# A fused decoder block: two heads share 32 rows of turned queries and keys, and the heads' outputs are packed by DMA and divided there

## The chip, the cores and the metric

The kernel runs on one core of one Trainium2 chip. The metric is the device time of one execution in microseconds (us), the median of several. A core has TensorE (PE in the profile, with its weight loads as PEld), VectorE (DVE), ScalarE (ACT), GpSimd (POOL) and SyncE (SP), which here only issues DMAs. Each engine works through its own instructions in order and waits at semaphores.

## The reference

One decoder block on 16 sequences of 256 tokens, width 256, 16 heads of 16, all in f32:

```python
# self-attention
k = layernorm_per_head(x @ Wk.T); q = layernorm_per_head(x @ Wq.T); v = x @ Wv.T
q, k = q * 256**-0.25, k * 256**-0.25
att = softmax(causal(q k^T));  x1 = layernorm(x + (att v) @ Wo.T + bo)
# cross-attention: queries of x1, keys and values of ctx, RoPE on q and k
att = softmax(Q K^T / sqrt(16));  x2 = layernorm(x1 + (att V) @ Wo + bo)
# mixture of 8 experts, 2 chosen per token, then the last layernorm
top2 = top_k(x2 @ router.T); y = sum(p_e * (gelu(x2 @ w1_e + b1_e) @ w2_e + b2_e))
```

## The kernel before

The kernel is written by hand, engine by engine, with explicit semaphores. Attention runs over 32 blocks: blocks 0 to 15 are the sequences' self-attention, 16 to 31 their cross-attention. Time is counted in quarters `q`; a block has four, and each engine's program is one loop over `q` with a fixed list of steps for each `r = q % 4`. The table of constants near L46 says how many quarters after a block's start each of its steps stands (`block_at`, `group_at`); several blocks are in flight at once. So the order of work on each engine is written out and does not depend on times.

One quarter handles one group of four heads. PE computes that group's scores (`score`), the weighted values of an earlier group (`weigh`) and the turned scores of another (`score_T`), from which ACT takes the exponentials (`weights`). DVE takes the maxima of the scores, in two halves (`maxima`, L1075); PE may not begin the next score before both are taken, nor the quarter's turned score before the first. PE reads the scores' operands from `qkT`, where the queries and keys lie turned (features on rows), 32 rows to a head, 16 of them used and one more for the maximum (queries) or a 1 (keys). To get there the rows of `qkn` are scaled (`scale_heads`) or rotated (`rotate`, `sum_turn`, `lay_out`) into the padded tile `pad`, then turned by PE in four jobs of four transposes (`turn_qk`, L645) and drained by ACT (`drain_turned`).

The values carry a column of ones, so `weigh` gives each head's outputs with their sum in row 16 of its 32 rows. PE turns these back (`turn_o`, L655, eight transposes), DVE inverts the sums and multiplies (`divide`, L1204 and L1208), PE turns the result again (`turn_on`, L669, four transposes), ACT drains it, and PE projects it (`project_o`, L681). DVE then adds the residual (L1219).

Most PE results go through two PSUM banks used in turn (the ring, `ring_places`); a job waits until the job two before it is drained. SP issues all plain DMAs on one queue: the maxima into `qkT` (`lay_max`, L382, four a block), the inputs (`load_xin`, `load_xb`), and in blocks 2 to 13 the zero rows of the experts' buffer (`lay_pads`, L392, two copies of 1,496 KB a block). POOL masks, adds biases and scatters the tokens; its tables for RoPE's bias are made at the start (`prepare_rope`). Behind the last block stand the experts (L792, L803), which the change does not touch.

Of the kernel before, what the change touches and what calls it, by code (L numbers as in the profile page):

```python
# [73 lines left out]
def ring_places():  # L74
# [7 lines left out]
    for q in range(QUARTERS):  # L82
        r = q % 4
        if r == 0:
            place("maxT", block_at(q, MAXT_AT))
            n = block_at(q, QK_AT)
            place("x1T", n, n is not None and crossed(n))
        elif r == 1:
            place("k23", block_at(q, TURN_K23))
        elif r == 2:  # L90
            place("o0", block_at(q, OUT_AT))
        else:
            place("onT", block_at(q, PROJECT_AT))
# [3 lines left out]
        elif r == 1:  # L97
            place("q23", block_at(q, TURN_Q23))
            place("qk1", block_at(q, QK_AT + 1))
        elif r == 2:  # L100
            place("o1", block_at(q, OUT_AT))
            place("v", block_at(q, V_AT))
            place("q01", block_at(q, TURN_Q01))
            n = block_at(q, TURN_X2)
            place("x2T", n, n is not None and crossed(n))
        else:
            place("k01", block_at(q, TURN_K01))
# [11 lines left out]
def decoder_block(nc, x, xT, ctxT, wqk_self, wv_self, wo_self, wq_x, wk_x, wv_x, wo_x, bo_self, bo_x,  # L119
# [4 lines left out]
    with ExitStack() as ctx:  # L124
# [30 lines left out]
        gv = sb("gv", [P, 4])  # L155
        cs = sb("cs", [P, 2, NT, 2, D])
# [8 lines left out]
        big = sb("big", [P, KC * NE * F])  # L165
        qkT = big[:, 0:6144].rearrange("p (b q g t) -> p b q g t", b=3, q=2, g=NG)
        pad = big[:, 6144:8192].rearrange("p (t q h d) -> p t q h d", t=NT, q=2, h=H)
# [10 lines left out]
        on = sb("on", [P, NT, E])  # L178
        onT = sb("onT", [P, KC, T])
# [3 lines left out]
        rec = sb("rec", [P, NT, H])  # L183
# [57 lines left out]
        bqk = pflat[:, 512:512 + 2 * E].rearrange("p (q e) -> p q e", q=2)  # L241
        bv = pflat[:, 1024:1024 + E]
        bvT = pflat[:, 1280:1280 + E].rearrange("p (c t) -> p c t", c=KC)
        gb = pflat[:, 1536:1536 + 2 * NT * 2 * D].rearrange("p (a t q d) -> p a t q d", a=2, t=NT, q=2)
        gp = pflat[:, 1792:1792 + 4 * P].rearrange("p (j i d) -> p j i d", j=4, i=GRP)
        turned_bias = pflat[:, 2304:2304 + 2 * E].rearrange("p (q e) -> p q e", q=2)
# [12 lines left out]
        early_in, late_in = sem("early_in"), sem("late_in")  # L259
# [3 lines left out]
        gp_ready, gp_pe, gv_ready = sem("gp_ready"), sem("gp_pe"), sem("gv_ready")  # L263
# [43 lines left out]
        def bc(ap, n):  # L307
            return ap.unsqueeze(len(ap.shape)).to_broadcast(list(ap.shape) + [n])
# [1342 lines left out]
```

## Time and profile before

| | |
|---|---|
| median of 3 runs | 1244.41 us (1242.04 to 1250.48) |
| the profiled execution | 1243.51 us, span 1241.8 us, mean granted clock 0.926 |
| PE busy | 1096.5 us, 88% |
| DVE busy | 801.8 us, 65% |
| ACT busy | 575.2 us, 46% |
| POOL busy | 274.3 us, 22% |
| attention, self blocks at full pace | about 78 to 348 us |
| attention, cross blocks at full pace | about 430 to 790 us |
| experts and last layernorm | from about 915 us |

Busy time is the sum of an engine's instructions; the span goes from the first to the last instruction of the execution. A share of the whole span mixes stages, so the table by stage and the timelines of single blocks tell more than the total. Registers, branches and the issuing of DMAs are not counted as busy. The granted clock is given as a share of TensorE's full speed.

### The profile page before, as it was taken

To read this page: it belongs to the slowest core of one execution; us is meant where nothing else is said; L and a number is where in the kernel's file an instruction comes from. 1 tells how busy PE (TensorE), PEld (TensorE's weight loads), DVE (VectorE), ACT (ScalarE), POOL (GpSimd) and SP (SyncE) were. 2 spreads that over 40 slices of the span, in tenths; PEclk is the share of its full clock that TensorE was granted. 3 is DMA by queue.
4 is the path that set the end of the run, shared out by engine and by line. 5 is a ranking of instruction groups with operands and counts; after the bars stand their busy time and mean duration, and the time that the engine had idled before them with its cause. 6 is when DMAs were issued, how large, how long until landed. Compare 5 with 4: busy or idle time off the path is not lost.

```text
span 1241.8 us, 29875 instructions
## 1 busy us (share of the span) xinstructions
PE 1096.5 (88%) x11181; PEld 801.0 (65%) x11181; DVE 801.8 (65%) x1935; ACT 575.2 (46%) x937; POOL 274.3 (22%) x311
## 2 busy tenths in 40 slices
PE   5899999999999899999999999888539999999920
PEld 3456666666666666666666666555439999999920
DVE  5647777778788787687777786753624444444447
ACT  2356666666655555555455554544212222222214
POOL 4022223232222200003030302202132222222210
PEclk9889999999999999999899998876669999999975
DMA  6104644635531000101010100001057767777654
GB/s 229 63 22 160 203 150 143 201 126 183 169 118 29 10 11 19 44 10 48 10 46 11 47 15 33 29 11 38 22 173 209 211 220 213 212 220 214 194 235 188
DMA packets 94651, 139.31 MB, mean 112 GB/s; under 512 B 11216, under 2 KB 68944, under 8 KB 93104
## 3 DMA queue, kind: packets, MB, share of 16 engines
q1 hardware_dynamic: 87888, 114.98, 29.8%
q0 software_dynamic: 6624, 22.42, 4.7%
q8 instruction: 93, 1.52, 0.5%
q14 instruction: 46, 0.38, 0.1%
HBM read 76.56 MB, written 60.29 MB: 110 GB/s over the span
## 4 chain that ended last, share of the span: by engine, by line
PE 75%; DVE 14%; issue 5%; ACT 3%; DMA 2%; POOL 1%; SPq 1%; ACTq 0%; POOLq 0%; DVEq 0%
PE PS L792 10%; PE PS L803 10%; PE PS L534 9%; PE PS L555 8%; PE PS L645 5%; PE PS L503 5%; PE PS L614 4%; PE PS L610 4%; DVE part L1075 3%; PE PS L681 3%; PE PS L628 2%; PE PS L510 2%; PE PS L655 2%; PE PS L669 2%; PE PS L506 2%
## 5 line engine op out<-in xcount | busy, mean ns | idle before, releaser
L1075 DVE TENSOR_REDUCE part<-PS 128x6 f32<-128x768 f32 (+1 forms) x256 | 272.5, 1087 | 114.2 <-PE PS L510 65.2
L871 ACT ACTIVATE pT<-PS 128x768 f32<-128x768 f32 (+1 forms) x256 | 220.8, 914 | 96.7 <-PE PS L534 96.7
L1536 POOL TENSOR_SCALAR_AFFINE_SELECT pT<-pT 128x512 f32<-128x512 f32 x128 | 87.6, 689 | 294.2 <-ACT pT L871 291.2
L534 PE MATMUL PS<-big 17*128 17x256 f32 (+1 forms) x2048 | 142.0, 393 | 9.7 <-DVE part L1075 6.6
L792 PEld LDWEIGHTS PS<-oT,big 128*128 128x128 f32 x1136 | 139.3, 194 | 5.2 <-ACT oT L982 1.6
L555 PE MATMUL PS<-pT,vaug 128*32 128x256 f32 (+1 forms) x2048 | 130.9, 375 | 12.0 <-DVE sq L1178 4.6
L792 PE MATMUL PS<-oT,big 128*128 128x128 f32 x1136 | 139.9, 277 | 1.0 <-ACT oT L982 1.0
L534 PEld LDWEIGHTS PS<-big 17*128 17x128 f32 x2048 | 98.7, 194 | 57.7 <-DVE part L1075 28.2
L803 PE MATMUL PS<-w2s,qkn 128*128 x568 | 134.4, 380 | 0.0
L1553 POOL DMA_INDIRECT xs_dram<-rows_all,posi x64 | 64.3, 1004 | 298.8 <-DVE posi L1331 282.9
L982 ACT ACTIVATE oT<-PS 128x256 f32<-128x256 f32 x71 | 27.2, 383 | 192.5 <-PE PS L781 192.5
L1572 POOL DMA_INDIRECT p_dram<-pT,rowid x71 | 68.1, 959 | 209.7 <-DVE rowid L1433 202.4
L803 PEld LDWEIGHTS PS<-w2s,qkn 128*128 128x128 f32 x568 | 102.4, 190 | 11.3 <-issue 0.3
L555 PEld LDWEIGHTS PS<-pT,vaug 128*32 128x32 f32 x2048 | 57.2, 112 | 60.3 <-issue 35.3
L882 ACT ACTIVATE oT<-PS 128x256 f32<-128x256 f32 x128 | 49.0, 383 | 98.9 <-PE PS L555 98.4
L1417 DVE TENSOR_TENSOR qkn<-PS,b1T 128x512 f32<-128x512 f32 x71 | 49.1, 691 | 65.2 <-PE PS L792 65.2
L645 PE MATMUL PS<-ident,big 128*128 128x128 f32 x512 | 84.5, 289 | 6.7 <-DVE on L1208 4.2
L1427 DVE TENSOR_TENSOR pT<-PS,w_self 128x256 f32<-128x256 f32 x71 | 30.1, 424 | 87.8 <-PE PS L803 87.8
L503 PE MATMUL PS<-big 16*128 16x256 f32 x1024 | 76.3, 413 | 9.4 <-ACT big L916 6.1
L645 PEld LDWEIGHTS PS<-ident,big 128*128 128x128 f32 x512 | 55.0, 143 | 42.7 <-issue 32.3
L614 PE MATMUL PS<-w_self,xin 128*128 128x512 f32 x128 | 68.4, 664 | 1.7 <-DVE w_self L1017 1.3
L503 PEld LDWEIGHTS PS<-big 16*128 16x128 f32 x1024 | 48.0, 190 | 27.4 <-ACT big L916 11.9
(166 smaller groups left out, 1603.6 us busy)
## 6 DMA issues: line engine op xcount, KB each, us to landing
big<-w SPq DMA_DIRECT2D x71, 512.0 KB
xs_dram<-zrow SPq DMA_DIRECT2D x24, 1496.0 KB, 9.0
oT<-xs_dram SPq DMA_DIRECT2D x71, 136.0 KB, 3.5
xin<-xT SPq DMA_DIRECT2D x16, 256.0 KB, 2.8
w2s<-w POOLq DMA_DIRECT2D x1, 4096.0 KB, 12.9
xb<-x SPq DMA_DIRECT2D x16, 256.0 KB, 10.6
xin<-ctxT SPq DMA_DIRECT2D x16, 256.0 KB, 2.8
big<-p_dram SPq DMA_DIRECT2D x4, 1024.0 KB, 7.9
```

The lines of the kernel that those rows point to most:

```text
L503: ins = pe.matmul(o, q, a[r0:r0 + D, 1, g, :], start=True, stop=True)
L534: ins = pe.matmul(o, keys, a[r0:r1, 0, g, q0:T], start=True, stop=True)
L555: ins = pe.matmul(o[PADDED * i:PADDED * (i + 1), q0:T], vaug[:, n % 4, kt, GRP * g + i, :], pT[:, k % 2, i, kt * T:kt * T + T - q0], start ...
L614: ins = pe.matmul(o, a[:, c, t * P:(t + 1) * P], w_qk[:, c, :], start=(c == 0), stop=(c == KC - 1))
L645: ins = pe.transpose(ring_slot(job)[:, j * T + t * P:j * T + (t + 1) * P], src, ident[:])
L792: ins = pe.matmul(moe_bank(1, j % 2)[:, f * P:(f + 1) * P], w1s[:, j % W1_BUFFERS, c, f * P:(f + 1) * P], xsT[:, j % 2, c * P:(c + 1) * P] ...
L803: ins = pe.matmul(moe_bank(3, j % 2)[:, 0:E], hact[:, j % 2, c * P:(c + 1) * P], w, start=(c == 0), stop=(c == FC - 1))
L871: act.activation(pT[:, k % 2, 2 * half:2 * half + 2, 0:wide], src, ACT.Exp).then_inc((exp_a, exp_b)[half], 1)
L1075: dve.tensor_reduce(dst, src, AX.X, ALU.max, negate=True).then_inc((max_a, max_b)[half], 1)
L1536: pool.affine_select(d, d, [[0, 2], [0, 2], [1, P]], ALU.is_ge, 0.0, base=0, channel_multiplier=-1).then_inc(masked, 1)
L1553: pool.indirect_dma_start(out=xs_dram, out_offset=bass.IndirectOffsetOnAxis(ap=posi[:, batch_index(last), c:c + 1], axis=0), in_=rows_all[ ...
L1572: pool.indirect_dma_start(out=p_dram, out_offset=bass.IndirectOffsetOnAxis(ap=rowid[:, o, 0:1], axis=0), in_=ye[:, o], in_offset=None).the ...
```

## The change

Queries and keys are now turned without padding: 16 heads of 16 fill 128 rows twice, so four transposes turn the queries of a block and four its keys (`turn_qk` reads `qkn` itself). Two heads share each strip of 32 rows. ACT drains each turned bank twice, once for each of the two heads of a strip, with a factor per row that is 1 (or the gain) on the head's own 16 rows and 0 on the other's (`within`, `gvb`); the keys get a 1 on one of the other's rows (`beyond`), and the maximum goes there in the queries. `score` contracts 32 rows.

The two transposing steps of the outputs and ACT's drain between them are gone. SP packs the outputs by 16 DMAs a block (`pack`): eight bring the 16 output rows of each head into a dense tile `packed[:, 0]`, eight bring the 16 rows of its sums (the ones columns give the sum in rows 16 to 31 alike) into `packed[:, 1]`. DVE inverts and multiplies there (`divide`), and the projection reads the tile as it is.

Some steps move: `divide` to quarter 3, the residual to the next quarter 0, `scale_heads` to quarter 1, `sum_turn` to quarter 2, `lay_out` to quarter 3, `turn_x1` three quarters earlier. At the start, the values' projection waits for four loads (`mid_in`), the bias tables are made later, and ACT no longer waits for them.

```diff
-QK_AT, V_AT, SQUARE_AT, VAR_AT, CHAIN_AT, SCALE_AT = 0, 2, 2, 3, 4, 6
-TURN_Q01, TURN_K01, TURN_Q23, TURN_K23 = 6, 7, 9, 9
-SUM_AT, LAY_AT = 3, 6
+QK_AT, V_AT, SQUARE_AT, VAR_AT, CHAIN_AT, SCALE_AT = 0, 2, 2, 3, 4, 5
+TURN_X1, TURN_Q, TURN_K = -3, 6, 7
+SUM_AT, LAY_AT = 2, 3
-OUT_AT, PROJECT_AT, LN_AT = 18, 19, 21
+PACK_AT, PROJECT_AT, LN_AT = 16, 19, 21
...
+            def pack(n, b):
+                if n is None:
+                    return
+                if b == 0 and n >= 1:
+                    await_filled(sp, ("wo", n - 1))
+                for g in range(2 * b, 2 * b + 2):
+                    await_drained(sp, ("pv", (n, g)))
+                for k in range(2):
+                    for i in range(GRP):
+                        r0, r1 = PADDED * i + D * k, PADDED * i + D * b
+                        sp.dma_start(packed[r1:r1 + D, k], oT[r0:r0 + D, n % 2, 2 * b:2 * b + 2, :]
+                                     ).then_inc(packed_in[n % 2], 16)
...
                 load_xb(block_at(q, MAXT_AT + 1))
+                pack(block_at(q, PACK_AT), 0)
+                pack(block_at(q, PACK_AT + 1), 1)
                 n = block_at(q, MAXT_AT)
                 if n is not None:
                     lay_pads(n)
...
             def project_o(n):
-                await_drained(pe, ("onT", n))
+                pe.wait_ge(divided, n + 1)
...
             def drain_turned(...):
+                for b in range(2):
+                    dst = qkT[:, n % 3, qk, 2 * b:2 * b + 2, :].rearrange("p g t -> p (g t)")
+                    if crossed(n):
+                        factor, term = within[:, b:b + 1], beyond[:, b:b + 1] if qk else none[:]
+                    else:
+                        factor, term = gvb[:, 0, b, qk:qk + 1], gvb[:, 1, b, qk:qk + 1]
+                    ins = act.activation(dst, ring_slot(job), ACT.Identity, bias=term, scale=factor)
+                ins.then_inc(drained_by(job), 1)
...
-            def divide(n, t):
+            def divide(n):
                 if n is None:
                     return
-                job = (("o0", "o1")[t], n)
-                await_filled(dve, job)
-                m = ring_slot(job).rearrange("p (h d) -> p h d", d=PADDED)
-                dve.reciprocal(rec[:, t, :], m[:, :, D]).then_inc(rec_ready, 1)
-                dve.wait_ge(rec_ready, next(n_rec))
-                if t == 0 and n >= 1:
-                    await_filled(dve, ("onT", n - 1))
-                dve.tensor_tensor(on[:, t, :].rearrange("p (h d) -> p h d", d=D), m[:, :, 0:D],
-                                  bc(rec[:, t, :], D), ALU.mult).then_inc(drained_by(job), 1)
+                dve.wait_ge(packed_in[n % 2], 256 * (n // 2 + 1))
+                dve.reciprocal(packed[:, 1], packed[:, 1]).then_inc(inverted, 1)
+                dve.wait_ge(inverted, n + 1)
+                dve.tensor_tensor(packed[:, 0], packed[:, 0], packed[:, 1], ALU.mult).then_inc(divided, 1)
...
                 if r == 0:
+                    residual(block_at(q, PROJECT_AT + 1))
...
                 elif r == 2:
                     maxima(group_at(q, SCORE_AT), 0)
-                    divide(block_at(q, OUT_AT), 0)
                     maxima(group_at(q, SCORE_AT), 1)
-                    scale_heads(block_at(q, SCALE_AT))
-                    lay_out(block_at(q, LAY_AT))
-                    divide(block_at(q, OUT_AT), 1)
+                    for t in range(NT):
+                        sum_turn(block_at(q, SUM_AT), t)
                     choose_second(block_at(q, SECOND_AT))
                 else:
                     maxima(group_at(q, SCORE_AT), 0)
                     maxima(group_at(q, SCORE_AT), 1)
                     combine(block_at(q, MAXT_AT - 1))
+                    divide(block_at(q, PROJECT_AT))
                     variances(block_at(q, VAR_AT))
-                    for t in range(NT):
-                        sum_turn(block_at(q, SUM_AT), t)
-                    residual(block_at(q, PROJECT_AT))
+                    lay_out(block_at(q, LAY_AT))
                     combine_weights(block_at(q, RANK_AT))
```

Three places of the resulting order follow. PE, quarters 2 and 3 of a self-attention block. Before (L655 and L669 turn outputs, L645 queries and keys, L628 projects values, L681 outputs):

```order
L510 MATMUL PS<-big 128x256 x4
L655 MATMUL PS<-ident,oT 128x128 x4
L555 MATMUL PS<-pT,vaug 32x256 x4
L555 MATMUL PS<-pT,vaug 32x128 x4
L534 MATMUL PS<-big 128x256 x4
L534 MATMUL PS<-big 128x128 x4
L655 MATMUL PS<-ident,oT 128x128 x4
L628 MATMUL PS<-w_self,xin 128x256 x4
L645 MATMUL PS<-ident,big 128x128 x4
L494 MATMUL PS<-identb,strips 128x2x32 x16
L506 MATMUL PS<-big 128x128 x4
L510 MATMUL PS<-big 128x256 x4
```

Now (L661 turns queries, L645 projects values):

```order
L529 MATMUL PS<-big 128x256 x4
L661 MATMUL PS<-ident,qkn 128x128 x4
L574 MATMUL PS<-pT,vaug 32x256 x4
L574 MATMUL PS<-pT,vaug 32x128 x4
L553 MATMUL PS<-big 128x256 x4
L553 MATMUL PS<-big 128x128 x4
L645 MATMUL PS<-w_self,xin 128x256 x4
L512 MATMUL PS<-identb,strips 128x2x32 x16
L525 MATMUL PS<-big 128x128 x4
L529 MATMUL PS<-big 128x256 x4
```

Three groups of four transposes became one here; between the projection of the values and the next score none is left.

DVE, from quarter 2 of a self-attention block to the next quarter 0. Before (L1204 and L1208 divide, L1152 sums the squares, L1219 is the residual):

```order
L1075 TENSOR_REDUCE part<-PS 128x2x3
L1204 RECIPROCAL rec<-PS 128x16
L1208 TENSOR_TENSOR on<-PS,rec 128x256
L1075 TENSOR_REDUCE part<-PS 128x2x3
L1141 TENSOR_TENSOR big<-qkn,chain 128x32x16 x2
L1204 RECIPROCAL rec<-PS 128x16
L1208 TENSOR_TENSOR on<-PS,rec 128x256
L1075 TENSOR_REDUCE part<-PS 128x2x3 x2
L1082 TENSOR_TENSOR part<-part 128x16
L1152 TENSOR_REDUCE vv<-sq 128x64
L1219 TENSOR_TENSOR y<-PS,xb 128x512
```

Now:

```order
L1133 TENSOR_TENSOR qkn<-qkn,chain 128x512 x2
L1070 TENSOR_REDUCE part<-PS 128x2x3 x4
L1077 TENSOR_TENSOR part<-part 128x16
L1188 RECIPROCAL packed<-packed 128x512
L1190 TENSOR_TENSOR packed<-packed 128x512
L1142 TENSOR_REDUCE vv<-sq 128x64
L1200 TENSOR_TENSOR y<-PS,xb 128x512
```

The scaling moved ahead of quarter 2's maxima, and one division of 512 columns stands behind the four maxima of quarters 2 and 3.

SP's queue, one self-attention block with zero rows. Before:

```order
L382 DMA big<-nmaxT 1x4x256 x4
L392 DMA xs_dram<-zrow 128x11x272 x2
L375 DMA xb<-x 128x2x256
L367 DMA xin<-xT 128x2x256
```

Now:

```order
L388 DMA big<-nmaxT 4x256 x4
L400 DMA packed<-oT 16x512 x8
L410 DMA xs_dram<-zrow 128x11x272 x2
L380 DMA xb<-x 128x2x256
L400 DMA packed<-oT 16x512 x8
L372 DMA xin<-xT 128x2x256
```

Eight packing copies stand ahead of the zero rows and eight behind them and `xb`.

## Rows read from the trace of the kernel before

**Rows 1.** Table by stage: us, busy us per engine, PEclk, DMA share, GB/s.

```profile
250.00:350.00 100.00, 98.97 (x1386) 64.84 (x1386) 76.56 (x151) 66.86 (x107) 30.22 (x41) 1.00 0.46 150
600.00:700.00 100.00, 95.17 (x942) 65.07 (x935) 73.51 (x180) 52.70 (x81) 21.36 (x20) 0.97 0.11 35
```

**Rows 2.** Timeline of PE, self-attention block: start us, us, engine, line, what.

```profile
190.38 1.98 PE L614 MATMUL PS<-w_self,xin 128*128 128x512 f32 x4
...
204.22 0.29 PE L494 MATMUL PS<-identb,strips 32*128 32x64 bf16 x16
...
205.18 0.66 PE L669 MATMUL PS<-ident,on 128*128 128x128 f32 x4
...
207.42 0.66 PE L645 MATMUL PS<-ident,big 128*128 128x128 f32 x4
207.91 1.89 PE L681 MATMUL PS<-w_self,onT 128*128 128x256 f32 x8
209.83 0.30 PE L494 MATMUL PS<-identb,strips 32*128 32x64 bf16 x16
...
212.81 0.70 PE L614 MATMUL PS<-w_self,xin 128*128 128x512 f32 x1
```

**Rows 3.** Timeline of DVE, the same block.

```profile
191.60 0.49 DVE L1112 TENSOR_SCALAR chain<-vv 128x66 f32<-128x66 f32 x1
...
193.84 1.82 DVE L1075 TENSOR_REDUCE part<-PS 128x6 f32<-128x768 f32 x2
...
197.52 0.60 DVE L1130 SCALAR_TENSOR_TENSOR shift<-vv,chain 128x2 f32<-128x2 f32 x1
...
211.81 0.88 DVE L1227 BATCH_NORM_STATS2 bst<-y 128x6 f32<-128x256 f32 x2
```

**Rows 4.** Groups on DVE, by shape: xcount | busy us, mean ns | idle.

```profile
L1185 DVE TENSOR_TENSOR qkn<-qkn,sq 128x512 f32<-128x512 f32 x32 | 20.9, 695 | 0.0
...
L1204 DVE RECIPROCAL rec<-PS 128x16 f32<-128x16 f32 x64 | 15.9, 248 | 17.8 <-PE PS L655 17.7
...
L1292 DVE RECIPROCAL prob<-odds 128x4 f32<-128x4 f32 x7 | 1.2, 178 | 0.2
...
L1292 DVE RECIPROCAL prob<-odds 128x2 f32<-128x2 f32 x2 | 0.3, 166 | 0.1
```

**Rows 5.** Timeline of PE, cross-attention: two successive blocks' first rows.

```profile
675.09 1.13 PE L610 MATMUL PS<-wx_q,x1T 128*128 128x256 f32 x4
...
702.88 1.13 PE L610 MATMUL PS<-wx_q,x1T 128*128 128x256 f32 x4
```

**Rows 6.** Timeline of DVE in that block: rotation and the maxima behind it.

```profile
677.17 0.69 DVE L1176 TENSOR_TENSOR qkn<-PS,cs 128x512 f32<-128x512 f32 x1
...
678.44 2.34 DVE L1075 TENSOR_REDUCE part<-PS 128x4 f32<-128x1024 f32 x2
```

**Rows 7.** Table by stage, slices of 1 us in a self-attention block.

```profile
192.00:193.00 1.00, 1.00 (x33) 0.63 (x32) 0.93 (x3) 0.63 (x2) 0.67 (x2) 1.00 0.33 119
202.00:203.00 1.00, 1.00 (x6) 0.87 (x6) 1.00 (x3) 0.98 (x2) 0.66 (x1) 1.00 0.45 147
```

**Rows 8.** One line's instructions, L375 (the loads of xb): issue to landing.

```profile
DMA to landing us min/median/max: 2.8/10.6/11.3
```

**Rows 9.** Timeline of SP's queue: the copies of the maxima, as issued.

```profile
211.62 1.86 SPq L382 DMA_DIRECT2D big<-nmaxT  x3
```

**Rows 10.** Timeline of PE at idles, and in the last block.

```profile
427.85 0.86 PE L555 MATMUL PS<-pT,vaug 128*32 128x256 f32 x16 [1.91 <-DVE sq L1178]
...
791.40 1.15 PE L503 MATMUL PS<-big 16*128 16x256 f32 x16 [1.34 <-DVE part L1075]
...
797.76 1.96 PE L503 MATMUL PS<-big 16*128 16x256 f32 x16 [1.96 <-ACT big L916]
...
881.70 3.78 PE L681 MATMUL PS<-wx_o,onT 128*128 128x256 f32 x8 [0.69 <-ACT onT L854]
```

**Rows 11.** Timeline of ScalarE at the start.

```profile
21.80 0.60 ACT L903 ACTIVATE vaug<-PS 128x512 f32<-128x512 f32 x1 [6.40 <-POOLq L1510]
```

More of the change, by code:

```diff
@@ L85, in ring_places @@
             place("maxT", block_at(q, MAXT_AT))
[L86 to L89, printed above, removed]
         elif r == 2:
-            place("o0", block_at(q, OUT_AT))
-        else:
-            place("onT", block_at(q, PROJECT_AT))
+            place("qT", block_at(q, TURN_Q))
+        elif r == 3:
+            place("kT", block_at(q, TURN_K))
         place("pv", group_at(q, WEIGH_AT))
@@ L275, in decoder_block @@
         masked = sem("masked")
-        rec_ready = sem("rec_ready")
+        packed_in = sems("packed_in", 2)
+        inverted, divided = sem("inverted"), sem("divided")
         xb_ready, y_link = sem("xb_ready"), sem("y_link")
@@ L308, in bc, with head @@
             return ap.unsqueeze(len(ap.shape)).to_broadcast(list(ap.shape) + [n])
+        def head(g, i):
+            b, c = divmod(g, 2)
+            return 8 * c + 2 * i + b
         def ring_slot(job):
@@ L380, in lay_max @@
                 await_drained(sp, ("maxT", n))
-                for i in range(GRP):
-                    sp.dma_start(qkT[PADDED * i + D:PADDED * i + D + 1, n % 3, 0],
-                                 nmaxT[GRP * i:GRP * i + GRP, :]).then_inc(max_in, 16)
+                for g in range(NG):
+                    first = D if g < 2 else 0
+                    sp.dma_start(qkT[first:P:PADDED, n % 3, 0, g], nmaxT[g:H:NG, :]).then_inc(max_in, 16)
+            def pack(n, b):
[10 more added lines that the diff above has]
+                                     ).then_inc(packed_in[n % 2], 16)
             def lay_pads(n):
@@ L399, in _ @@
             load_xin(0)
-            for dst, src in ((small[:], tables), (w_v, wv_self), (gb[:, 0], gains), (gb[:, 1], shifts),
-                             (w_o, wo_self), (wx_q[:], wq_x), (wx_k[:], wk_x), (wx_v[:], wv_x),
-                             (wx_o[:], wo_x), (bo[:, 0], bo_self), (bo[:, 1], bo_x), (bqk[:, 0], bq_x),
+            for dst, src in ((small[:], tables), (w_v, wv_self), (gb[:, 0], gains), (gb[:, 1], shifts)):
+                sp.dma_start(dst, src).then_inc(mid_in, 16)
+            load_xin(1)
+            for dst, src in ((w_o, wo_self), (bo[:, 0], bo_self), (wx_q[:], wq_x), (wx_k[:], wk_x),
+                             (wx_v[:], wv_x), (wx_o[:], wo_x), (bo[:, 1], bo_x), (bqk[:, 0], bq_x),
                              (bqk[:, 1], bk_x), (bv, bv_x), (cs[:], rope), (rw[:], router)):
                 sp.dma_start(dst, src).then_inc(late_in, 16)
-            load_xin(1)
             for q in range(QUARTERS):
@@ L630, in project_v, with turn_qk @@
                 ins.then_inc(filled_by(job), 1)
-            def turn_qk(name, n, qk, half):
+            def turn_qk(name, n, qk):
                 if n is None:
@@ new lines, in prepare @@
+                dve.wait_ge(gv_taken, 1)
+                for b in range(2):
+                    dve.tensor_scalar(gvb[:, 0, b], gv[:, 0:2], within[:, b:b + 1], None, ALU.mult)
+                    dve.tensor_scalar(gvb[:, 1, b, 0:1], gv[:, 2:3], within[:, b:b + 1], None, ALU.mult)
+                    ins = dve.tensor_scalar(gvb[:, 1, b, 1:2], gv[:, 3:4], within[:, b:b + 1], beyond[:, b:b + 1],
+                                            ALU.mult, ALU.add)
+                ins.then_inc(gv_ready, 1)
```

242 lines of the change are left out of this document (97 added, 145 removed).

## The prediction, written before the changed kernel was run

> **What bounds the kernel now.** I read the table by stage first. In the self-attention stage TensorE (PE) is busy 98.97 of 100 us at full clock, VectorE (DVE) 76.56; in the cross-attention stage 95.17 and 73.51 [rows 1]. So both stages run at PE's pace, and DVE has about a quarter of its time free. The timeline of PE gives the pace: one block of self-attention takes 22.43 us (from 190.38 to 212.81, [rows 2]), one of cross-attention 27.79 us [rows 5]. A block is four quarters; each has one score group, one weighing and one turned score group, and fixed extra work. Between the blocks' 12 full self periods (78 to 348 us) and 13 full cross periods (430 to 790 us) lie 3 mixed ones. The expert part after 915 us is not touched.
>
> **What goes.** Each block loses 20 of its 28 PE transposes of 128x128: 8 of 16 for queries and keys, 8 of the outputs, 4 of the divided outputs. Four of them take 0.49 us behind a turned score group (207.42 to 207.91, [rows 2]) and about 0.6 behind a score. So 5 x 0.55 = 2.7 us, PE's own work falling to 19.7 us in a self block. The score matmuls contract 32 rows for 16; their columns stay, and I cost that at nothing: they take the same row strips, and the 17-row turned scores run at the 16-row ones' pace. If PE stayed saturated, 28 x 2.7 would be 76 us. ScalarE gains a second pass over each turned bank and loses one drain; it has 30% free and I cost it at nothing while PE waits elsewhere.
>
> **What comes: the division.** Before, DVE inverted 16 sums per partition, twice a block, 248 ns each, and multiplied 256 elements [rows 4]. Now the sums lie in a 128x512 tile, each repeated over the rows of its head, and one reciprocal inverts all 512 per partition. The trace has no such size. Its small ones are 166 ns for 2 elements, 178 for 4 and 248 for 16 [rows 4]: 5.8 to 6 ns per element, while an ordinary operation takes 695 ns for 512 [rows 4], near 1 ns. The bounds are 0.7 us (a reciprocal streams like any operation, the slope being start-up) and 7.9 us (16 to 512 in proportion). I take the straight line through the three rows: 0.15 + 512 x 0.0058 = **3.15 us**, and 0.7 for the multiplication: 3.85 us, where 1.34 stood.
> The Trainium skill, in "VectorE: DVE Perf Modes", section "First, the fixed hardware budget", says that reciprocal is an iterative divide with a repeat count of 8. The trace agrees with an iterative operation; eight cycles per element would be more than its rows give, and is a rival below.
>
> **Where it lands.** The division stands in quarter 3, behind both maxima of that quarter's scores, and the output projection of the same quarter waits for it. I lay out a self block from the start of quarter 3's score (t=0), with steps from [rows 2] and [rows 3].
> PE: score to 0.96; turn, weigh, turned score (as 205.18 to 207.42) to 3.2; then it needs the division.
> DVE: two maxima (193.84 to the next step, 1.73) from 1.1 to 2.85, combining to 3.0, reciprocal to 6.15, multiplication to 6.85. PE waits **3.7 us**. Projection (1.92, 207.91 to 209.83) to 8.8.
> Then DVE's residual waits for that projection (8.9 to 9.6), and its queue is a chain: score maxima of quarter 0 (from 9.95), moments 1.3, second maxima, first half of the rsqrt chain 2.24 (191.60 to 193.84) to 15.25; the first maxima of quarter 1 end at 16.1. PE, after score and weighing of quarter 1, would start its turned score at 15.45, so it waits 0.75. DVE: second maxima, rest of the chain 2.55 (to the end of 197.52's row), scaling 1.25, to 20.8. PE is at the query turn at 19.9 and waits 0.95. The rest runs at PE's pace; quarter 3 begins again at 24.95. A self block without other delay: 19.7 + 3.7 + 0.75 + 0.95, or 24.95 by the layout: **25.0 us, +2.6**.
> Cross block: the same wait is 0.1 + 2.27 (two maxima, 678.44 onwards) + 3.85 - 2.67 (PE's turn, weigh, turned score) = 3.6; in quarter 1 DVE's queue (moments, chain, rotation 1.27, from 677.17 to 678.44, [rows 6]) makes PE wait about 1.1. 27.8 - 1.2 (small idles before) - 2.7 + 3.6 + 1.1 = 28.6, **+0.8**; 13 of them 10 us. The 3 mixed ones: +0.5 each.
>
> **The copies that pack.** 16 DMAs a block are added on SP's queue, 8 in quarter 0 ahead of the zero rows (two copies of 1.5 MB, 12 self blocks have them), 8 in quarter 1 behind these and behind xb. SP's issues take 0.62 us apiece and the four of the maxima start 1.8 us after quarter 0 (211.62 against 209.83, [rows 2, 9]). So the zero rows start at 1.8 + 12 x 0.62 = 9.2. They fill the DMA engines for 10 us (eleven slices from 192 to 203, the nine between at 1.0, [rows 7]), and xb, issued behind them, lands after 10.6 us in the median against 2.8 when alone [rows 8]: the queue works in turn. So the zero rows end at about 19.6, xb and the last eight copies (256 KB each) at about 22.2. DVE reaches the division at 16.15 + 3.0 = 19.1. It waits 3.1, then 3.85 and the projection: a block of **28.0 us, +5.6**, 12 of them 67 us. Bounds of this wait: nothing (a block of 25.0) and 10 us (queue full, all issues held back). In cross blocks nothing is ahead; the copies land near 16 of a needed 22.
>
> **The clock.** PE now idles 3.7 us and more in one piece in every block. Before, of five idles of 1.7 us or more outside the last part (ending at 20.1, 32.2, 70.7, 427.8 and 797.8), four were followed by the lower level (1.2 GHz), as before 797.76, where an idle of 1.96 us made a score of 1.15 us take 1.96 (791.40 and 797.76, [rows 10]); one of 1.91 us at 427.85 was not [rows 10]. The stretches lasted 3 to 21 us. If it falls, the projection costs 1.9 more (3.78 for 8 matmuls at 881.70, [rows 10]), the next score 0.9, in cross blocks the logits 0.9: 3.3 on average, all on the path. Bounds 0 and 3.3 a block; I take 0.7 x 3.3 = 2.3, since idles are longer than those of the rows: 28 x 2.3 = 64 us.
>
> **The ends.** At the start ScalarE no longer waits 6.4 us for POOL's rope tables [rows 11], and the first value projection waits for 4 late loads, not 16: -9 (-5 to -13). At the end the last block's 8 copies (5.0), their landing (2.8) and 3.85 stand where 12 transposes and two drains stood: +6 (0 to 12).
>
> **Sum.** 67 + 10 + 1.5 + 64 - 9 + 6 = +140 on the profiled execution's 1243.5, so 1383. The median of the runs shown is 1244.4, 1 us above; no difference to the forecast. One per cent, 12 us, is what a measurement can tell from no change.
>
> **Rivals and chances.**
> A, the forecast, 0.60: **1383**, its own range 1340 to 1430.
> B, 0.14: all waits come, but the clock stays up. For it: from 82 to 600 us the granted clock hardly fell; against it: those blocks had no idle of 2 us. 1243.5 + 76 = 1319.
> C, 0.08: the packed copies are not held up by the zero rows. For it: they are small and many rings may let them by; against: xb's landing. 12 x 3.1 less: 1346, or 1282 with the clock up too.
> D, the other side, 0.10: the reciprocal streams at about 1 ns per element. Place: quarter 3's division; price 0.7 for 3.15 us. PE's wait falls from 3.7 to 1.2 and the block to 22.5 (self) and 26.1 (cross), and with idles that short the clock stays. With the copies in time: 0 + 13 x (-1.7) - 3 and the mixed blocks -6, about 1212; with them late (+3.1 in 12 blocks) 1249. For it: three rows of tiny size are thin evidence; against: all three lie on one line, with six times the slope of any other operation. Leaving the clock out, it decides the sign from about 1.8 us for the reciprocal downwards. 0.06 for the first, 0.04 for the second.
> E, 0.06: eight cycles per element. A cycle is what an ordinary operation needs per element, (695 - 166)/510 = 1.04 ns [rows 4], so 0.15 + 512 x 8.3 ns = 4.4 us, 1.2 more in 28 blocks: 1383 + 34 = 1417. Against: the rows say 5.6 cycles. The Trainium skill, "VectorE: DVE Perf Modes", can be read so.
> F, 0.02: the change pays in full, 2.7 us a block and 9 at the start: 1244 - 85 = 1159. It needs a division that hides; nothing on PE stands between.
> Range: B's 1319 and E's 1417 are in, D, F and half of C out: **1300 to 1430**. Faster: D's first case and F, 0.08. Same: D's second, 0.04. Slower: 0.88.
>
> **What would show it.** Right: a 128x512 reciprocal near 3.15 us; PE's largest wait on the projection, released by DVE's multiplication, 3 to 4 us in cross blocks and 6 to 7 in self blocks; DVE waiting for packed copies in blocks 1 to 12 alone; granted clock at 0.5 after those idles; self blocks of 28 to 31 us and cross blocks near 31. Wrong: a reciprocal below 2 us, periods under 22.4 and 27.8, or packed copies landing before the maxima end. A clock that stays at 1.0 gives B.

## The result and the profile after

| | before | after |
|---|---|---|
| median | 1243.22 us (1237.72 to 1250.48, 4 runs) | 1403.43 us (1401.06 to 1410.35, 4 runs) |
| profiled span | 1241.8 us | 1402.0 us |
| mean granted clock | 0.926 | 0.878 |
| PE busy | 1096.5 us | 1053.8 us |
| DVE busy | 801.8 us | 889.3 us |

The change makes the kernel slower: the ratio is 1.1281, 95% interval [1.1241, 1.1321], where 1383 us and a range of 1300 to 1430 were forecast. PE has less to do and the kernel still takes 160 us more, so the loss is idle time and low clock. The table by stage of the kernel after, same stretches and columns as [rows 1] (the stretch, its length, busy us of PE, PEld, DVE, ACT, POOL, then the granted clock, DMA share and GB/s):

```profile
250.00:350.00 100.00, 65.53 (x870) 40.75 (x870) 60.92 (x97) 42.80 (x69) 19.92 (x28) 0.84 0.42 128
600.00:700.00 100.00, 83.33 (x780) 57.27 (x781) 74.83 (x143) 45.48 (x68) 3.82 (x3) 0.90 0.13 36
```

In self-attention PE falls from 98.97 to 65.53 busy us of 100 and DVE falls too, so neither is the bound: they wait for each other. The waits of the kernel after name the place (engine, line, whom it waited for; us in total, times, longest):

```profile
PE PS L674 <- DVE packed L1190: 187.0, 31, 12.0
...
DVE y L1200 <- PE PS L674: 74.5, 32, 3.7
...
DVE packed L1188 <- DMA packed<-oT: 76.1, 15, 10.6
```

PE waits before each projection (L674) for the multiplication (L1190), 6 us on average. DVE itself waits before the reciprocal (L1188) for the copies in 15 blocks: 59.2 of the 76.1 us are in the twelve blocks with zero rows, 4.9 each, 0.8 in one more, and 16.1 in the last two blocks of all, where no later block is left to work on. One such block, first on DVE, then on PE, then on SP's queue (start, duration; in brackets the idle before and what ended it):

```profile
342.38 1.82 DVE L1070 TENSOR_REDUCE part<-PS 128x6 f32<-128x768 f32 x2 [3.60 <-PE PS L529]
344.31 0.17 DVE L1077 TENSOR_TENSOR part<-part 128x16 f32<-128x16 f32 x1
348.67 3.35 DVE L1188 RECIPROCAL packed<-packed 128x512 f32<-128x512 f32 x1 [4.19 <-DMA packed<-oT]
352.06 0.69 DVE L1190 TENSOR_TENSOR packed<-packed 128x512 f32<-128x512 f32 x1
352.67 1.21 DVE L1142 TENSOR_REDUCE vv<-sq 128x64 f32<-128x1024 f32 x1
```
```profile
343.60 0.94 PE L553 MATMUL PS<-big 32*128 32x256 f32 x16
352.81 3.55 PE L674 MATMUL PS<-w_self,packed 128*128 128x256 f32 x8 [8.27 <-DVE packed L1190]
356.29 0.30 PE L512 MATMUL PS<-identb,strips 32*128 32x64 bf16 x16
```
```profile
334.22 1.47 SPq L410 DMA_DIRECT2D xs_dram<-zrow  x2
335.74 3.59 SPq L380 DMA_DIRECT2D xb<-x  x1
339.43 7.84 SPq L400 DMA_DIRECT2D packed<-oT  x8
```

Read backwards, the chain is this: the projection starts at 352.8 because the multiplication ended then, this because of 3.35 us of reciprocal, and this because the last copies landed at 348.7, after SP had issued the eight of them from 339.4 to 347.3. The zero rows fill the DMA engines until about 344 (their share is 1.03 to 1.08 in the slices of 2 us from 336 to 344), but from 346 to 348 it is 0.28 and the last of the eight are still being issued: the copies end with their issuing. Behind the zero rows and `xb` one issue takes 0.98 us, where sixteen in a cross block took 0.63 each (10.03 us from 548.13). The projection then takes 3.55 us where it took 1.92 [rows 2]. The table by stage of this stretch shows the clock (columns as above, the clock third from the end):

```profile
345.00:349.00 4.00, 0.00 (x0) 0.00 (x0) 0.33 (x1) 1.12 (x2) 2.53 (x3) 1.00 0.36 90
349.00:350.00 1.00, 0.00 (x0) 0.00 (x0) 1.00 (x1) 0.00 (x0) 0.00 (x0) 0.58 0.56 191
350.00:356.00 6.00, 3.19 (x8) 2.50 (x8) 3.85 (x3) 0.00 (x0) 0.00 (x0) 0.50 0.01 3
356.00:358.00 2.00, 2.00 (x44) 1.02 (x46) 1.29 (x2) 0.32 (x1) 0.00 (x0) 1.00 0.01 4
```

Behind its idle PE is at the lower level (0.50, 1.2 GHz), and it is back at the higher one (2.4 GHz) as the projection ends; only the projection pays. A cross block has the same without the copies: idle 3.80 us, projection 3.57 us.

```profile
754.38 3.34 DVE L1188 RECIPROCAL packed<-packed 128x512 f32<-128x512 f32 x1
757.76 0.69 DVE L1190 TENSOR_TENSOR packed<-packed 128x512 f32<-128x512 f32 x1
```
```profile
753.56 1.15 PE L553 MATMUL PS<-big 32*128 32x256 f32 x16
758.51 3.57 PE L674 MATMUL PS<-wx_o,packed 128*128 128x256 f32 x8 [3.80 <-DVE packed L1190]
```

To place the 160 us I took, in each kernel, the starts of ScalarE's drain of the turned maxima (one per block) and their distances. S is the mean of the ten distances in self-attention from block 3 to 13, C that of the thirteen in cross-attention from 17 to 30; "to block 3" runs from the span's start, "last" from block 31's drain to the end.

| | to block 3 | S | 13 to 17 | C | 30 to 31 | last | span |
|---|---|---|---|---|---|---|---|
| before | 121.5 | 22.43 | 103.0 | 28.31 | 31.2 | 393.8 | 1241.8 |
| after | 131.9 | 32.31 | 123.4 | 30.61 | 26.3 | 399.4 | 1402.0 |

So of +160: 10 x 9.88 = 99 in these self blocks, 10 up to block 3, 20 from block 13 to 17 (the mixed blocks and the self blocks beside them), 13 x 2.30 = 30 in cross blocks, -5 and +6 at the end.

### The profile page after: what moved, and what is told of

It reads as the page before. It is cut to its first block, busy times and chain, and to the rows that moved or that the text cites. A ratio compares the mean times of both kernels' runs of the same rounds, so it can differ in the third digit from the quotient of the medians.

```text
span 1402.0 us, 28744 instructions
## 1 busy us (share of the span) xinstructions
PE 1053.8 (75%) x10541; PEld 766.7 (55%) x10541; DVE 889.3 (63%) x1879; ACT 560.1 (40%) x905; POOL 265.8 (19%) x309
## 4 chain that ended last, share of the span: by engine, by line
PE 52%; DVE 29%; SPq 8%; issue 5%; DMA 4%; ACT 2%; POOL 0%; DVEq 0%; ACTq 0%; POOLq 0%
PE PS L785 9%; PE PS L796 9%; PE PS L674 8%; DVE part L1070 8%; DVE packed L1188 7%; SPq L400 7%; PE PS L522 5%; PE PS L553 4%; PE PS L574 4%; PE PS L627 3%; PE PS L645 3%; DMA packed<-oT 2%; DVE packed L1190 2%; PE PS L661 1%; DVE qkn L1133 1%
## 5 line engine op out<-in xcount | busy, mean ns | idle before, releaser
L553 PE MATMUL PS<-big 32*128 32x256 f32 (+1 forms) x2048 | 137.5, 383 | 31.5 <-issue 28.3
L1516 POOL TENSOR_SCALAR_AFFINE_SELECT pT<-pT 128x512 f32<-128x512 f32 x128 | 81.8, 639 | 413.0 <-ACT pT L851 409.1
L1188 DVE RECIPROCAL packed<-packed 128x512 f32<-128x512 f32 x32 | 107.1, 3348 | 76.1 <-DMA packed<-oT 76.1
L674 PE MATMUL PS<-w_self,packed 128*128 128x256 f32 x128 | 58.8, 639 | 125.1 <-DVE packed L1190 125.1
L553 PEld LDWEIGHTS PS<-big 32*128 32x128 f32 x2048 | 96.6, 189 | 77.2 <-issue 45.9
L818 ACT ACTIVATE nmaxT<-PS 16x256 f32<-16x256 f32 x32 | 11.9, 373 | 301.7 <-PE PS L589 301.7
L674 PEld LDWEIGHTS PS<-w_self,packed 128*128 128x128 f32 x128 | 40.2, 329 | 137.0 <-DVE packed L1190 128.3
L964 ACT ACTIVATE oT<-PS 128x256 f32<-128x256 f32 x71 | 27.3, 384 | 194.1 <-PE PS L774 194.1
L674 PE MATMUL PS<-wx_o,packed 128*128 128x256 f32 x128 | 52.7, 585 | 61.9 <-DVE packed L1190 61.9
L522 PE MATMUL PS<-big 32*128 32x256 f32 x1024 | 79.9, 429 | 6.3 <-ACT pT L851 5.0
```

What stands on the lines that cost most here:

```text
L522: ins = pe.matmul(o, q, a[r0:r1, 1, g, :], start=True, stop=True)
L553: ins = pe.matmul(o, keys, a[r0:r1, 0, g, q0:T], start=True, stop=True)
L674: ins = pe.matmul(ring_slot(job)[:, t * E:(t + 1) * E], packed[:, 0, c, t * P:(t + 1) * P], w[:, c, :], start=(c == 0), stop=(c == KC - 1))
L1188: dve.reciprocal(packed[:, 1], packed[:, 1]).then_inc(inverted, 1)
L1516: pool.affine_select(d, d, [[0, 2], [0, 2], [1, P]], ALU.is_ge, 0.0, base=0, channel_multiplier=-1).then_inc(masked, 1)
```

## The experiments

Twelve kernels ran. With the first eight the kernel before took 1270.5 and 1267.7 us in place of 1243, with the last four 1244.4 and 1246.9; so each is told by its ratio to the kernel before beside it, and S and C are from its profile. Three of them, e1_plain, e3_both and e9_late_plain, leave the inversion of the sums out, so their outputs are not the block's; their instructions are otherwise the same, with the same 71 expert tiles.

C is less safe than S: `e2_zero_last` differs from the kernel after in nothing that runs in a cross block, and its C is 33.85 against 30.61. Its trace shows where most of that lies. In the profiles of the first eight kernels ScalarE has 10 to 14 idles of up to 6.4 us, all in cross-attention behind block 17, that no event of the core ended (the profile says "remote"), as here in e2_zero_last:

```profile
661.84 0.38 ACT L863 ACTIVATE oT<-PS 128x256 f32<-128x256 f32 x1 [4.36 <-remote]
```

They sum to 1.9 to 3.0 us per cross block, 2.98 in e2_zero_last, and the profiles of the kernel before, the kernel after and the last four have none. What they are is not shown; they came with the runs in which the kernel before was slower too, though it has no profile there. S has none of them. C is compared between kernels of one group alone, and with these idles in mind.

| kernel | ratio, 95% interval | S | C |
|---|---|---|---|
| after | 1.1281 [1.1241, 1.1321] | 32.31 | 30.61 |
| e1_plain | 1.0351 [1.0262, 1.0441] | 29.41 | 28.51 |
| e2_zero_last | 1.0889 [1.0793, 1.0984] | 27.32 | 33.85 |
| e3_both | 0.9697 [0.9608, 0.9786] | 22.83 | 28.23 |
| e4_turn_only | 1.0206 [1.0117, 1.0296] | 25.07 | 31.47 |
| e5_fill | 1.0452 [1.0409, 1.0495] | 25.47 | 31.09 |
| e6_late | 1.0225 [1.0194, 1.0255] | 24.65 | 30.28 |
| e8_slots | 1.0051 [1.0016, 1.0086] | 22.97 | 31.28 |
| e9_late_plain | 0.9635 [0.9593, 0.9676] | 22.12 | 27.78 |
| e10_slots_scale | 0.9851 [0.9813, 0.9890] | 22.84 | 27.87 |
| e11_spread | 0.9765 [0.9723, 0.9806] | 22.68 | 26.66 |
| e12_spread_slots | 1.0131 [1.0092, 1.0170] | 22.77 | 29.23 |
| e14_spread_residual | 0.9689 [0.9653, 0.9726] | 22.72 | 26.03 |

### The reciprocal, the zero rows, and both

```diff
 # e1_plain, and in e3_both
-dve.reciprocal(packed[:, 1], packed[:, 1])
+dve.tensor_scalar(packed[:, 1], packed[:, 1], 1.0, None, ALU.mult)
 # e2_zero_last, and in e3_both: behind pack(block_at(q, PACK_AT + 1), 1)
-n = block_at(q, MAXT_AT)
+n = block_at(q, MAXT_AT + 1)
 if n is not None:
     lay_pads(n)
```

e1_plain. 

> The changed kernel with an ordinary multiplication by 1 in place of the reciprocal (so the sums are not inverted). Theory (the division's length is on the path of every block): DVE's step falls from 3.35 to 0.7 us or less, 2.7 in each of 31 blocks, about 85 us; PE's idle in cross blocks falls from 3.8 to about 1.1 and the clock stays up there, another 20 to 30: 1285 to 1300. The late copies stay in the self blocks. Rival (the reciprocal only fills time in which PE waits for something else): less than 40 us, 1365 or more.

e2_zero_last. 

> The changed kernel, only that the zero rows are issued behind the second eight packing copies, not ahead of them. Theory (the copies wait in SP's queue behind the zero rows): DVE's wait of 76 us for packed copies goes, self blocks fall from 32 to 27 or 28 us, 1325 to 1340. Rival (16 copies a block are late by their own issuing, 0.6 us and more each): the wait stays over 40 us, 1370 or more.

e3_both. 

> Both edits together (no inversion of the sums, zero rows last). Theory: 76 and 85 us go and the clock stays up, which gives 40 to 60 more: 1190 to 1215, below the kernel before. Rival (other parts of the change cost too: the second drains, 32-row scores): 1244 or more.

Measured 1319.2, 1388.9 and 1234.4 us beside 1270.5 of the kernel before. By their ratios, on the 1243.2 us of the kernel before in the result, that is 1287, 1354 and 1206: the first and the third lie in their theories' ranges. The second lies 14 us above its own and 16 below its rival's, though its self blocks fell to 27.3 as the theory said. Without the long reciprocal a self block is 2.9 us shorter, without the copies' delay 5.0, without both 9.5: more than the sum, because only then the clock stays up (one matmul of the self-attention projections has a median of 634 ns in e1_plain and in e2_zero_last, and 379 in e3_both). With zero rows last, DVE's wait for the copies is gone from self-attention (15.6 us of it stay in the last two blocks of all) and PE's wait shrinks (the kernel e2_zero_last):

```profile
PEld PS L675 <- DVE packed L1191: 17.2, 4, 4.3
PE PS L675 <- DVE packed L1191: 16.5, 4, 4.1
```

These are the waits from 250 to 350 us, 4.1 us a block, where the kernel after has 28.6 in three. With both gone the self block is at 22.83 us, 0.4 from the kernel before, and the whole is faster than it. So these two and what they do to the clock are the loss in self-attention.

### The clock by itself

```diff
+# e5_fill: e2_zero_last, and on PE ahead of project_o
+pe.wait_ge(max_b, NG * u[0] + u[1] + 1)
+for _ in range(20):
+    pe.transpose(bank(0)[:, 0:P], ident[:], ident[:])
 project_o(n)
```

> The second kernel with the zero rows issued behind the second eight copies, as in e2_zero_last (1.089 of the kernel before), and one addition: behind the score groups PE waits for the maxima and then turns the identity matrix 20 times into a bank of scores, ahead of its wait for the packed outputs. These results are read by nobody. Theory (the idle of 4 to 8 us ahead of the projection lowers PE's clock for the projection and what follows, about 1.7 to 2 us a block): the projection's matmul falls from a median of 634 ns towards 380 and the time by 28 x 1.7 = 48 us, to a ratio of 1.05. Rival (the clock falls after the added work all the same, because the rest of the wait is long enough, or the low clock lies under waits): within 10 us of e2_zero_last, a ratio of 1.08 to 1.10. If the added turns push the wait out instead of filling it, over 1.10.

Measured 1321.8 us, 67 us under e2_zero_last; the ratio fell by 0.044 to 1.045, and the theory had 1.05. Twenty useless turns in each block make the kernel faster. One block of e5_fill on PE:

```profile
237.98 2.40 PE L757 MATMUL PS<-ident 128*128 128x128 f32 x20
242.16 1.99 PE L675 MATMUL PS<-w_self,packed 128*128 128x256 f32 x8 [1.78 <-DVE packed L1197]
```

The wait ends at the same event, but only 1.78 us of it are idle in one piece and the projection takes 1.99 us. Over all projections of self-attention, minimum, median and maximum of one matmul, first in the kernel after, then in e5_fill:

```profile
L674 PE MATMUL PS<-w_self,packed x128: 380/634/796, 90.6 to 575.5; 128*128 128x256 f32 x128
```
```profile
L675 PE MATMUL PS<-w_self,packed x128: 379/379/483, 89.4 to 482.9; 128*128 128x256 f32 x128
```

S fell from 27.32 to 25.47. So the clock costs **1.85 us** a self block. And 27.32 - 22.83 (e2 to e3) is 4.49. The multiplication by 1 that stands for the reciprocal takes 0.42 us, 2.93 less than the reciprocal; with 1.85 for the clock that would be 4.78. The two experiments agree within 0.3 us.

### The shared rows alone

e4_turn_only keeps the shared rows, the doubled drains and the new start, and turns and divides the outputs as before:

```diff
-PACK_AT, PROJECT_AT, LN_AT = 16, 19, 21
+OUT_AT, PROJECT_AT, LN_AT = 18, 19, 21
 # PE, quarters 2 and 3, ahead of weigh
 turn_qk("qT", block_at(q, TURN_Q), 0)
+turn_o(block_at(q, OUT_AT), 0)
 ...
 turn_qk("kT", block_at(q, TURN_K), 1)
+turn_on(block_at(q, PROJECT_AT))
```

> One part of the change alone: shared 32 rows with two drains, and the new start, but the outputs turned and divided as before. Theory: 8 transposes of 16 go, 1.1 us a block, 31 us, and 9 at the start: 1200 to 1210, 3% faster than before. Rival (32-row scores and the second drains cost): 1235 or more.

Measured 1301.5 us, ratio 1.021: my theory fell, and the rival's time came. PE and ScalarE of this kernel in quarter 2:

```profile
202.45 0.66 PE L650 MATMUL PS<-ident,qkn 128*128 128x128 f32 x4 [0.66 <-DVE qkn L1160]
202.95 0.60 PE L661 MATMUL PS<-ident,oT 128*128 128x128 f32 x4
204.74 0.86 PE L563 MATMUL PS<-pT,vaug 128*32 128x256 f32 x16 [1.19 <-ACT big L928]
```
```profile
203.15 1.45 ACT L928 ACTIVATE big<-PS,gvb 128x512 f32<-128x512 f32 x2 [0.71 <-PE PS L650]
```

The ring has two banks. The weighing is the second job after the queries' turn, so it needs the bank that ScalarE now reads twice, 1.45 us, and there is only 0.60 us of PE work in between. This wait came 54 times, 63.4 us. In the kernel after the weighing follows the turn directly and takes the other bank: the second drain is free there and not here.

e8_slots puts the turns where the kernel before has them, behind the projections; e10_slots_scale restores VectorE's order as well:

```diff
 # e8_slots, PE (ring and drains alike)
+project_v(...); turn_qk("qT", ..., 0)
+turn_qk("kT", ..., 1); project_o(...)
 # e10_slots_scale, DVE
-residual(block_at(q, PROJECT_AT + 1))   # r == 0
-scale_heads(block_at(q, SCALE_AT))      # r == 1, SCALE_AT 5
+scale_heads(block_at(q, SCALE_AT))      # r == 2, SCALE_AT 6
+residual(block_at(q, PROJECT_AT))       # r == 3
```

e8_slots. 

> The shared rows alone with the outputs turned and divided as in the kernel before (e4_turn_only, 1.021 of the kernel before), with the turns of the queries and keys put where the kernel before has its turns of heads 0 and 1: behind the projections of a quarter instead of ahead of the weighing, and their drains behind ScalarE's other drains. Theory (e4_turn_only lost its gain in the ring of two PSUM banks: the weighing waits about 1.19 us, 54 times, for a bank that ScalarE drains twice, 1.45 us instead of 0.5): the wait goes and with it 63 us and more; ratio 0.95 to 0.97. Rival (the scores on 64 rows or ScalarE's 0.9 us more a drain hold the block up anyway): 1.00 to 1.02. A third outcome: the keys' drain is now late for the scores of the next quarter, 1 us a block, ratio near 0.98.

e10_slots_scale. 

> The shared rows alone, outputs turned and divided as before, the turns of queries and keys in the slots of the kernel before (e8_slots, 1.005 of the kernel before), and VectorE's order put back too: the scaling of the heads stands in the third quarter, between the second maxima and the second division, instead of behind the second quarter's maxima, and the residual in the quarter of its projection. Theory (in e8_slots the chain of waits runs over VectorE: maxima, the chain of the inverse root, the scaling of 1.2 us and then the next maxima, for which PE waits): ratio 0.95 to 0.98, so that the shared rows by themselves are a gain. Rival (the 8 turns saved a block are no bound because ScalarE's doubled drains take their place): 1.00 to 1.01, as e8_slots.

Measured: ratios 1.005 and 0.985. In e8_slots the weighing's wait is gone from the list of waits and S fell by 2.1 us, but the ratio only by 0.016, some 20 us where 63 and more were expected: the theory fell and the rival's range came true. (Its scores contract 32 rows, not the 64 of that text.) e10_slots_scale lies between its theory's 0.95 to 0.98 and its rival's 1.00, nearer the theory: both missed. S is 22.84, no shorter than before's 22.43 with 8 turns fewer, and PE is busy 93 of 100 us there. Its gain lies in the cross blocks and the ends. The shared rows alone are worth 1.5%, and only with the order of the turns, the scaling and the residual as it was. C fell by 3.4 us from e8_slots to e10_slots_scale; part of this is e8_slots' idles from outside (2.7 us a cross block by their sum, not all of it on the path). Its blocks without such an idle take about 30.1 us against 28.3, so some 2 us are the edit's, and in a cross block only the residual's place is edited.

### The division off the chain

e6_late moves the projection and all behind it four quarters on, with two buffers and the zero rows last; e9_late_plain multiplies there instead; e11_spread cuts the reciprocal in four:

```diff
-PACK_AT, PROJECT_AT, LN_AT = 16, 19, 21
+PACK_AT, DIVIDE_AT, PROJECT_AT, LN_AT = 16, 19, 23, 25
-packed = sb("packed", [P, 2, KC, T])
+packed = sb("packed", [P, 2, 2, KC, T])
 # e11_spread: one piece at the end of each quarter's work, j = 0 to 3
+part_of = packed[:, n % 2, 1, j // 2, (j % 2) * P:(j % 2 + 1) * P]
+dve.reciprocal(part_of, part_of)
```

e6_late. 

> The second kernel with the division left where it stands on VectorE (4 quarters of a block ahead as before) but the projection, the residual, the norm and all that follows moved one block's worth of quarters (4) later, two buffers of packed outputs, and the zero rows issued behind the second eight copies. The reciprocal of 3.35 us stays, and nobody waits for it at once. Theory (the cost of the change is the chain copies, reciprocal, multiplication, projection inside one quarter, and the clock that it lowers; the removed transposes and the shared rows are a gain when that chain is off the path): faster than the kernel before, ratio 0.94 to 0.98, about as the second kernel with a multiplication for the reciprocal and the zero rows last (0.970), with PE's wait for the packed outputs gone and the granted clock above 0.93. Rival (VectorE with 3.3 us more a block, and ScalarE's doubled drains, bound it as they do the shared rows alone, 1.02): 1.00 to 1.03, with PE waiting for the maxima or for drains instead.

e9_late_plain. 

> e6_late with a multiplication by 1 in place of the reciprocal (the sums are not inverted). Theory (with the projection 4 quarters later the reciprocal is off the path): within 1% of e6_late, though VectorE is busy 2.6 us a block less. Rival (VectorE's queue is what the scores wait for, so 3.3 us in front of the next maxima is paid): 28 x 1 to 2.6 us, 2 to 6% faster than e6_late.

e11_spread. 

> e6_late (projection 4 quarters later, 1.0225 of the kernel before; with a multiplication for the reciprocal 0.9635) with the reciprocal cut into four pieces of 128 columns, 0.8 us each, one at the end of VectorE's work of each of the four quarters between the copies and the projection. Theory (the 3.3 us cost because they stand in one piece in front of the next group's maxima, for which PE waits; in pieces they fit into VectorE's idle time, 17 to 20 us of 100): ratio 0.97 to 1.00. Rival (VectorE's total work bounds the block, so a piece costs what it takes wherever it stands): 1.015 to 1.03, as e6_late.

Measured 1292.9, 1219.7 and 1214.7 us; ratios 1.022, 0.964, 0.976. For the first two my theory fell and the rivals' ranges came true; for e11_spread the theory did. PE does not wait for the division in e6_late's projections any more, and yet taking out the reciprocal gains 6%: S falls by 2.53 us of the 2.92 saved. The timeline of DVE of e6_late shows why:

```profile
303.42 1.82 DVE L1071 TENSOR_REDUCE part<-PS 128x6 f32<-128x768 f32 x2 [3.60 <-PE PS L530]
305.35 0.17 DVE L1078 TENSOR_TENSOR part<-part 128x16 f32<-128x16 f32 x1
305.44 3.35 DVE L1189 RECIPROCAL packed<-packed 128x512 f32<-128x512 f32 x1
308.82 0.82 DVE L1191 TENSOR_TENSOR packed<-packed 128x512 f32<-128x512 f32 x1
309.57 1.21 DVE L1143 TENSOR_REDUCE vv<-sq 128x64 f32<-128x1024 f32 x1
310.69 0.68 DVE L1201 TENSOR_TENSOR y<-PS,xb 128x512 f32<-128x512 f32 x1
311.29 0.94 DVE L1071 TENSOR_REDUCE part<-PS 128x6 f32<-128x768 f32 x1
```

From 305.4 to 311.3 DVE works without a gap, and only then takes the next maxima; before that it had idled 3.6 us. Nobody awaits the reciprocal itself, but somebody awaits the residual (L1201) that stands behind it: the residual frees the bank of the ring into which PE projected, and the weighing (L575), two jobs on, needs that bank. PE's largest wait of e6_late from 250 to 350 us says so, 2.7 us in each of four blocks:

```profile
PE PS L575 <- DVE y L1201: 10.9, 4, 2.7
```

Over the whole kernel this wait is 45.2 us, 1.8 us in e9_late_plain, and e11_spread has none of it. The queue is in order: what is off the chain by its data is on it by its place. In four pieces the work is even more (4 x 0.94 = 3.76 us), but no single piece stands long before an awaited step: DVE is busy 88.8 of 100 us from 250 to 350, S is 22.68, and the kernel is faster than the kernel before.

e12_spread_slots (the slots of e8_slots and SCALE_AT 6 on top), and e14_spread_residual, which only moves the residual back:

```diff
-residual(block_at(q, PROJECT_AT + 1))   # r == 0
+residual(block_at(q, PROJECT_AT))       # r == 3, ahead of combine_weights
```

e12_spread_slots. 

> e11_spread with the turns of queries and keys behind the projections of their quarters (as in e8_slots and the kernel before) and the scaling of the heads in the third quarter (as in e10_slots_scale). Theory (both orders hold VectorE's queue clear in front of the maxima): 1 to 3% under e11_spread, ratio 0.94 to 0.98, the fastest of all that compute the reference. Rival (with only one other job a quarter in the ring the slots don't matter, and VectorE is full): within 1% of e11_spread.

e14_spread_residual. 

> e11_spread (0.9765 of the kernel before) with the residual put back into the quarter of its projection, behind VectorE's other work of that quarter, instead of at the head of the next one. Theory (between e8_slots and e10_slots_scale a block of cross attention fell from 30.9 to 28.1 us and one of self attention from 23.4 to 23.1, and of the two edits only the residual's place touches cross attention): the blocks of cross attention fall from 26.7 towards 25.8 us, the ratio to 0.965 to 0.975. Rival (VectorE now stands waiting for the projection with nothing behind it that could run, and is 88% busy here against 75% there): no change within 0.5% or 1% slower.

e12_spread_slots missed both its theory and its rival: 1261.7 us, slower than e11_spread by 0.037. The keys' double drain now comes last in ScalarE's quarter, and the next scores (L511) and the logits (L685) wait for it (PE's waits of e12_spread_slots):

```profile
PE PS L511 <- ACT big L899: 15.5, 15, 2.4
...
PE PS L685 <- ACT big L899: 12.9, 11, 1.2
```

In e11_spread the first of these is 3.3 us. That is part of the loss and not all: the scores' waits are in self blocks, where S is no worse (22.77 against 22.68), and the logits wait 1.17 us a block where C rose by 2.57. What the rest is, no run separates. e14_spread_residual came as expected: 1208.2 us, ratio **0.969** [0.9653, 0.9726], the fastest that computes the whole block, C down from 26.66 to 26.03. Against e11_spread, [0.9723, 0.9806], the intervals just touch; that C fell by 0.63 us, 8 us in thirteen blocks, is what speaks for the step. In its two stages:

```profile
250.00:350.00 100.00, 87.71 (x1276) 56.05 (x1272) 88.65 (x164) 60.48 (x98) 29.06 (x39) 0.98 0.58 175
600.00:700.00 100.00, 90.46 (x954) 62.29 (x954) 92.17 (x204) 57.55 (x87) 22.06 (x20) 1.00 0.19 54
```

DVE is now the busier engine; the 20 turns saved on PE are paid for by 3.76 us of reciprocal on it.

## Why the prediction was right, step by step

- **What goes**: PE's busy time fell by 43 us, less than 2.7 x 32 = 86, since work at the low clock adds to it: the output projections alone went from 62.7 to 111.5 us. The step holds, but its two costs at nothing are not alike. The 32-row scores take what the 16-row ones took: the median of a score's matmul in cross-attention is 374 ns in the kernel before and after. The second drain at "nothing" is right in the kernel after and wrong as a rule: in e4_turn_only PE waited 63 us for it, and moving the turns took some 20 us off the time.
- **The division**: the line through three tiny sizes gave 3.15 us, measured 3.35, 6% more. The slope from 16 to 512 elements is 6.25 ns per element, six times the 1.04 ns of an ordinary operation in the kernel before. Rivals D (0.7) and E (4.4) are out. The Trainium skill, "VectorE: DVE Perf Modes", section "First, the fixed hardware budget", has reciprocal as an iterative divide with a repeat count of 8. A slope six times that of an ordinary operation fits an iterative one, but it is not eight of the 1.04 ns steps per element.
- **Where it lands**: 25.0 us were laid out for a self block without copies and clock; e5_fill, which is that block, has 25.47, of which 0.2 is the longer reciprocal. PE's wait was 3.7 by the layout; 3.80 in the cross block shown and 4.1 in e2_zero_last.
- **The copies**: the mechanism was right, and its size, 3.1 us, was 1.9 too small. The wait is 4.9 us in each of the twelve blocks with zero rows, and e2_zero_last gains 5.0 us a block. I had `xb` and the last eight land together, 13.0 us after the zero rows began to be issued (22.2 against 9.2). In the block shown the last copy landed 14.5 us after (348.7 against 334.2), since issuing went on so long: `xb` and the second eight took 11.5 us from first to last, where nine issues of 0.62 us make 5.6.
- **The clock**: 2.3 us a block was taken; 1.85 measured in self blocks. It fell nearly everywhere, as forecast: the median matmul of the projections took 634 ns, in self-attention as in cross-attention, where it had taken 379. The 0.7 in the forecast rested in part on a misreading: the idle of 1.91 us that ended at 427.85 was followed by the lower level too (0.50 in the slices from 430 to 432), so all five idles of the kernel before were, not four. What kept the cost under the full 3.3 us is that in the self block shown the lower level ends with the projection, and the next score is not slowed. Rival B, that it stays up, is out for this kernel.
- **The ends**: ScalarE's 6.4 us wait is gone, but of the -9 block 1's drain shows 4.2 (68.9 against 73.1) and block 2's 2.4; block 3 is 10 us late, behind the first block that the copies held up. From block 31's drain to the end it is +5.6 for +6.
- **The sum**: self blocks +9.9 for +7.9, cross blocks +2.3 for +3.1. The 20 us by which 1383 was short are made up so: ten self blocks +99 for +79, 20 too little, nearly all of it the copies (10 x 1.9); thirteen cross blocks +30 for +40, 10 too much; and the rest, with the start, two more self blocks, the mixed ones and the end, +31 for +21, 10 too little. That the number came within 20 us owes something to these errors cancelling; the kinds of cost and their order came as written.

What stays open: what the idles from outside are that lengthen the cross blocks of the first eight kernels, and so how much exactly of C's fall between e8_slots and e10_slots_scale is the residual; and where most of e12_spread_slots' loss in cross blocks comes from. A cheaper way to invert, say on fewer elements ahead of their spreading, was not tried.

## What to carry to other kernels

Price a moved operation by its elements per partition and by its own rate, then ask what stands behind it in its engine's queue: a long instruction with all the time in the world still delays the next one that somebody awaits, here a residual that frees a bank. Cutting it into pieces turned 2% lost into 2% won. When PE must idle anyway, count the clock as well as the wait; here twenty turns that nobody reads, put into the gap, paid for themselves. Small DMAs that a chain waits for go ahead of the large ones on their queue, and a second read of a shared bank is free only where the job two places on, which needs that bank, is far enough away.

## What the runs showed of the hardware

- A reciprocal over 512 f32 elements per partition takes 3.35 us on DVE, one over 128 takes 0.94, over 16 takes 0.25: about 6.2 ns an element and 0.15 us fixed. Multiplying 512 by 1 in place takes 0.42 us.
- Issuing a 32 KB DMA on SP's queue took 0.6 us with no large copy ahead, 0.98 on average and up to 1.96 us behind two copies of 1,496 KB.
- Twenty matmuls that nobody reads, in a wait of about 4 us, made the kernel 67 us faster, 1.85 us of it in each self block, with the granted clock held up (0.941 over the span where it had been 0.876).
